# L1 weights quantised tile by tile during the L0 stages; expert weights through a ring of two tiles

## The chip, the cores and the metric

The kernel runs on one core of one Trainium2 chip. The metric is the device time of one execution in microseconds (us), the median of three runs. Five engines work at once: TensorE (PE) multiplies and transposes, VectorE (DVE) and GpSimd (POOL) do elementwise work and reductions, ScalarE (ACT) does activations and copies, SyncE (SP) issues every DMA.

## The reference

A four-layer pre-norm decoder in fp32: batch 8, sequence 128, width 256, 16 heads. Each layer is an attention, a cross-attention (or another mixer) and a feed-forward part, each added to `x`. What matters here:

```python
# L0 feed-forward: hidden width 1024, plain fp32
gated = jax.nn.silu(x @ w_gate.T) * (x @ w_up.T);  out = gated @ w_down.T

# L1 feed-forward: weights and activations on shared exponents, blocks of 32
amax = max(abs(xb), axis=-1)                  # of one block of 32
scale = exp2(clip(floor(log2(amax)) - 2, -127, 127))
q = quantize_elem(xb / scale) * scale         # 2 exponent bits, saturated
out = _mx_linear(silu(_mx_linear(x, w_gate)) * _mx_linear(x, w_up), w_down)

# L2 feed-forward: 8 experts, the best 2 of each token, rank-32 additions
x1 = x @ W1.T + lora1;  x3 = x @ W3.T + lora3   # hidden width 896
x2 = silu(x1) * x3
out += (x2 @ W2.T + lora2) * rw[:, k:k + 1]     # k = 0, 1
```

The weights of the L1 feed-forward part are 1024x256, 1024x256 and 256x1024, 3 MB in all, and they depend on no activation: they can be quantised at any time after they are loaded.

## The kernel before

The work is cut into small **units** (`rows`, `cols`, `pv`, `gate0`, `mg` and so on), each with a part on one or more engines. Batches 0 to 3 form stream A, batches 4 to 7 stream B, loads and work on weights stream W. The twelve stages (L0, L0x, L0F, L1, L1x, L1F, L2, L2x, L2F, L3, L3x, L3F: attention, cross part and feed-forward of each layer) follow each other within a stream. `half()` lists the units of A or B, `weights()` those of W, and the string `TURNS` merges the three lists: `A3` takes the next three units of A, `a4` takes one that lies a few places ahead. Every engine runs its parts of all units in that one order and never out of it, so a unit that waits holds back everything behind it on that engine. Semaphores are counted by `Marks` (`inc`, `at`), buffers that are used in turn by `Ring` (`take` gives the next buffer and what must have ended, `done` frees it). `put` and `get` issue DMAs, all on SP's queue.

**L1 weight units.** `load l1f0`, `l1f1`, `l1f2` fetch the three weights into `wB` (10 DMAs, after `down L0F 3`, the last unit of the L0 feed-forward part: the space was that part's). `mxw(n, k)` quantises one of 12 tiles of 128x512 on DVE (`mx_quant`, ten instructions: a maximum over blocks, five small ones of 128x16, four of 128x512), then two additions on POOL (`mx_out`) round it to bf16, four transposes on PE (`mxw_t`) and a copy on ACT put it into `mgT`, `muT` or `mdT`. These units stand between those of the L1 attention of both halves. The scratch `mxw_w` holds one tile's two intermediates, the small rings `mxw_s`, `mxw_l` two tiles.

**Attention units.** A `rows` unit computes scores of 128x512 on PE (with the causal mask as a matmul with `cmask`) and their maxima on DVE (`negm`); `nm` sends the negated maxima by DMA into `stkA` or `stkB`; `cols` computes the scores again, transposed, with the maximum subtracted, for the exponential on ACT; `pv` multiplies by the values. For L0 the stacks are filled by `stack0` (queries or keys, DMA out of `scrq`, `scrk`) and `mrow` (the mask row out of `scrm`, which exists once `down L0 1` has run, and constant rows).

**L2 feed-forward units.** `w13(hf, f)` loads one tile of 512 KB (four DMAs: W1, W3, B1, B3 of 128 hidden units) into a ring of three tiles in `wB`, after `mxd 7`, the last product of the L1 part. `mg(hf, f)` multiplies with it (8 matmuls of 128x512, two records each in the trace), `ms(hf, f)` adds the second expert's difference and frees the tile. `w2` (896 KB) lies whole in `wA`, loaded by `l2n` after the L1 feed-forward part, and is read by `mw`.

## Time and profile before

| what | value |
|---|---|
| median of 3 runs | 1195.68 us (1198.04, 1195.68, 1180.78) |
| the profiled execution | 1184.46 us, its span 1182.6 us |
| PE busy | 972.1 us, 82% of the span |
| DVE busy | 769.7 us, 65% |
| ACT busy | 387.6 us, 33% |
| POOL busy | 295.8 us, 25% |
| DMA | 79.59 MB, mean 67 GB/s |

The profile is of one execution. Busy time is the time in which an engine had an instruction in it; PEclk is the clock that TensorE was granted, in tenths of full speed; in a row of the timeline the first number is the start, the second the duration, and in square brackets stands how long the engine had been idle and what ended it.

### The profile page before, as it was taken

What the parts mean: (1) busy time and instruction counts of PE and PEld (TensorE: products, weight loads), DVE (VectorE), ACT (ScalarE), POOL (GpSimd) and SP (SyncE); (2) the same over time, 40 slices, a digit from 0 to 9 for tenths busy, and PEclk for the clock granted to TensorE, in tenths of its full rate; (3) what the DMA queues carried; (4) which work ended last, traced back from release to release, by engine and by line L of the source; (5) the groups of instructions that cost most, each with busy time, mean ns of one, the idle gap of its engine ahead of it and who ended that gap; (6) DMA issues with size and microseconds to landing.
All of it is one profiled execution on the core that took longest, in us unless ns stands there. A gap on an engine that the chain in (4) does not pass through costs nothing.

```text
span 1182.6 us, 16030 instructions
## 1 busy us (share of the span) xinstructions
PE 972.1 (82%) x5874; PEld 577.6 (49%) x5878; DVE 769.7 (65%) x1764; ACT 387.6 (33%) x766; POOL 295.8 (25%) x314
## 2 busy tenths in 40 slices
PE   6677999999978676635736689999999999896778
PEld 3333344455745454313414554554644447584667
DVE  6783688424299899899789772523432214898786
ACT  2213477612135334413424341351212302413121
POOL 2420000101034243243023343112332322360520
PEclk9865699999999798766868789999999999998989
DMA  8686500001774445400170266112101140450001
GB/s 277 97 135 130 62 2 3 1 1 43 122 187 85 79 82 118 81 1 2 42 121 2 75 155 114 38 37 82 37 0 54 36 87 2 155 106 2 2 1 36
DMA packets 88065, 79.59 MB, mean 67 GB/s; under 512 B 8968, under 2 KB 86449, under 8 KB 87730
## 3 DMA queue, kind: packets, MB, share of 16 engines
q1 hardware_dynamic: 87986, 78.56, 31.4%
q8 instruction: 47, 0.77, 0.3%
q14 instruction: 32, 0.25, 0.1%
HBM read 62.41 MB, written 15.60 MB: 66 GB/s over the span
## 4 chain that ended last, share of the span: by engine, by line
PE 56%; DVE 28%; DMA 6%; issue 5%; ACT 3%; SPq 1%; POOL 1%; DVEq 0%; POOLq 0%; ACTq 0%
PE bank L562 52%; DVE negm L1406 5%; DMA stkA<-nm 2%; DMA stkB<-nm 1%; DMA stkA<-scrq 1%; PE bank L576 1%; PE bank L690 1%; SPq L1988 1%; ACT E L1126 1%; DVE hr L1327 1%; DVE nm L1426 1%; DVE oT L1806 1%; DVE nmb L1424 1%; DVE mxs L1569 1%; DVE stkB L1800 1%
## 5 line engine op out<-in xcount | busy, mean ns | idle before, releaser
L1406 DVE TENSOR_REDUCE negm<-bank 128x2 f32<-128x512 f32 (+1 forms) x256 | 163.0, 685 | 46.1 <-PE bank L562 44.6
L1126 ACT ACTIVATE E<-bank 128x512 f32<-128x512 f32 x256 | 140.7, 599 | 119.5 <-PE bank L562 117.9
L562 PE MATMUL bank<-hT,wB 128*128 128x512 f32 x272 | 126.0, 605 | 0.0
L1886 POOL TENSOR_TENSOR rstd<-ve,mhalf 128x2 f32<-128x2 f32 x48 | 35.1, 732 | 334.3 <-DVE ve L1319 334.2
L562 PE MATMUL bank<-stkA 96*128 96x128 bf16 (+5 forms) x768 | 93.8, 274 | 24.4 <-DMA stkA<-nm 14.0
L562 PE MATMUL bank<-E,vaug 128*32 128x128 f32 (+1 forms) x1536 | 97.7, 345 | 16.4 <-ACT E L1126 14.3
L562 PEld LDWEIGHTS bank<-stkA 96*128 96x128 bf16 (+5 forms) x768 | 61.6, 108 | 68.7 <-issue 32.2
L562 PE MATMUL bank<-stkB 96*128 96x128 bf16 (+5 forms) x768 | 83.4, 248 | 13.7 <-DMA stkB<-nm 5.4
L562 PEld LDWEIGHTS bank<-hT,wB 128*128 128x128 f32 x272 | 51.6, 194 | 60.1 <-issue 59.3
L562 PEld LDWEIGHTS bank<-stkB 96*128 96x128 bf16 (+5 forms) x768 | 57.8, 102 | 47.2 <-issue 21.9
L562 PE MATMUL bank<-wB 128*128 128x512 f32 x168 | 75.8, 594 | 0.0
L562 PE MATMUL bank<-hT,wA 128*128 128x512 f32 (+1 forms) x120 | 58.4, 638 | 2.1 <-ACT hT L1098 2.1
L1098 ACT COPY hT<-bank 128x512 f32<-128x512 f32 x36 | 21.0, 587 | 118.6 <-PE bank L576 118.6
L562 PEld LDWEIGHTS bank<-E,vaug 128*32 128x32 f32 x1536 | 33.9, 113 | 52.8 <-issue 23.3
L576 PE MATMUL bank<-ident,hr 128*128 128x128 f32 x144 | 24.5, 301 | 32.6 <-DVE hr L1327 32.6
L562 PEld LDWEIGHTS bank<-wB 128*128 128x128 f32 x168 | 31.4, 190 | 37.0 <-issue 36.8
L562 PE MATMUL bank<-stkA,wA 128*128 128x256 f32 (+1 forms) x152 | 47.8, 473 | 0.0
L1739 DVE TENSOR_TENSOR stkA<-E,bank 128x512 f32<-128x512 f32 x14 | 9.6, 687 | 57.9 <-PE bank L562 35.0
L562 PE MATMUL bank<-wA,oT 128*128 128x256 f32 (+2 forms) x192 | 43.5, 365 | 4.3 <-ACT oT L1149 3.3
L562 PE MATMUL bank<-stkB,wA 128*128 128x256 f32 (+1 forms) x152 | 47.0, 471 | 0.0
L562 PE MATMUL bank<-wB,oT 128*128 128x256 bf16 (+1 forms) x124 | 34.3, 439 | 14.2 <-DVE negm L1406 4.5
L1739 DVE TENSOR_TENSOR stkB<-E,bank 128x512 f32<-128x512 f32 x14 | 9.6, 688 | 55.3 <-PE bank L562 35.4
(302 smaller groups left out, 1846.2 us busy)
## 6 DMA issues: line engine op xcount, KB each, us to landing
scrq<-parts SPq DMA_DIRECT2D x20, 384.0 KB, 2.6
scrk<-parts SPq DMA_DIRECT2D x16, 384.0 KB, 2.8
wB<-in_l_w SPq DMA_DIRECT2D x28, 128.0 KB, 2.4
wB<-in_l_b SPq DMA_DIRECT2D x28, 128.0 KB, 2.4
stkA<-scrq SPq DMA_DIRECT2D x4, 768.0 KB, 8.8
stkA<-scrk SPq DMA_DIRECT2D x6, 512.0 KB, 9.8
stkB<-scrq SPq DMA_DIRECT2D x4, 768.0 KB, 8.6
stkB<-scrk SPq DMA_DIRECT2D x6, 512.0 KB, 9.4
```

Of the source, the lines that this page charges most:

```text
L562: return e.matmul(out, lhsT, rhs, start=start, stop=stop, skip_group_check=True)
L576: i = e.transpose(bk[:, k * 256 + c * 128:k * 256 + c * 128 + 128], HR.buf((L, p))[:, k, c * 128:c * 128 + 128], ident[:, :])
L690: i = e.transpose(bk[:, q * 128:q * 128 + 128], ut[:, s:s + 128], ident[:, :])
L1098: e.copy(hT_pair(hT, p), banks.buf(("feat", L, p))[:, :].rearrange("q (b c t) -> q b c t", b=2, c=2)).then_inc(*inc("hT", L, p))
L1126: e.activation(eb[:, :], banks.buf(("cols", L, b, u))[:, :], ACT.Exp, scale=8 ** -0.5 if L == "L0x" else 0.25).then_inc(*inc("exp", L, b, u))
L1327: e.tensor_scalar(hp[:, k, :], x[:, b, :], mv[:, b, 0:1], rstd[:, b:b + 1], ALU.subtract, ALU.mult).then_inc(*inc("norm", L, b))
L1406: e.tensor_reduce(ng[:, o:o + hp], banks.buf(("rows", L, b, u))[:, :].rearrange("p (h s) -> p h s", h=hp), AX, ALU.max, negate=True).then_ ...
L1424: e.tensor_copy(rb, r).then_inc(*inc("maxb", L, b))
L1426: e.tensor_tensor(nm[64:80, 0:n], r, rb, ALU.subtract).then_inc(*inc("maxl", L, b))
L1569: e.tensor_reduce(a, s3, AX, ALU.max, apply_absolute_value=True).then_inc(*inc("mxa", *key, 0))
L1739: e.tensor_tensor((X0, X1)[k][hf][:, f, :], eb[:, :], banks.buf(("mg", hf, f, 1))[:, :], ALU.mult).then_inc(*inc("xk", hf, f, k))
L1886: e.tensor_tensor(rstd[:, 2 * p:2 * p + 2], ve[:, 2 * p:2 * p + 2], mhalf[:, 2 * p:2 * p + 2], ALU.pow).then_inc(*inc("rstd", L, p))
```

## The change

- The loads `l1f0` to `l1f2` are gone. A new unit `l1f(n, k)` loads one tile of 256 KB into a ring `XW` of two tiles in `oT`, the buffer of the L0 cross-attention's context; it waits for the last readers of that context and for the tile's transposes. `mxw` reads the ring, `mx_out` writes into it, `mxw_t` frees it. The scratch lies in `oT` too, and the small rings have one entry each instead of two.
- In the merged order all 12 tiles move from the L1 attention to the end of the L0 cross-attention of B and the L0 feed-forward part of both halves. The order has been written anew throughout; other things in it move as well (the first stacks, the loads `l1a` and `l1x`, the int8 weights' units, ten `rows` of L1).
- `mgT`, `muT` lie at the end of `wB`, `mdT` in `wA`. ACT's copies into `oT` in L1 wait for the last tile, the `q8t` copies of the queries wait for `down L1`.
- `W13` is a ring of two tiles with memory of its own; `w13` and `a13` wait for `down L0F 3` instead of `mxd 7`. `w2` is no longer kept whole: it goes through the same ring for each half, as two units of 4 and 3 row blocks, and `mw` waits for them.

```diff
         steps += [[(u, bs[n - d]) for u in us] for d, us in ((0, ("x2s", "x2e")), (1, ("x2t",)), (2, ("x2o",))) if 0 <= n - d < 4]
     out["L2x"] = steps
-    steps = [[("w13", 0, f)] for f in range(3)] if hf == 0 else []
+    steps = [[("w13", hf, f)] for f in range(2)]
     steps += layernorm("L2F", ps) + [[("lg", hf), ("rt", hf)], [("lgT", hf)], [("mk", hf)]]
     steps += [[("ma", hf, n, c)] for n in range(2) for c in range(2)] + [[("mg", hf, 0)]]
     for f in range(1, 8):
         steps += ([[("mg", hf, f)]] if f < 7 else []) + [[("ms", hf, f - 1)]]
-        steps += [[("w13", hf, f + 2)]] if f < 5 else [[("w13", 1, f - 5)]] if hf == 0 else []
+        steps += [[("w13", hf, f + 1) if f < 6 else ("w2", hf, f - 6)]]
     steps += [[("ma2", hf, k, c)] for k in range(2) for c in range(2)] + [[("zf", hf, f)] for f in range(7)]
     out["L2F"] = steps + [[("mw", p)] for p in ps] + [[("mb", p)] for p in ps]
     out["L3"] = head("L3", hf) + attention("L3", bs)
...
-    out += [("L1", [("load", "l1a")])] + [("L1x", [("load", n)]) for n in ("l1x", "l1xb", "l1bq")]
-    out += [("L1x", s) for n in range(2) for s in ([("q8w", n)], [("q8w_t", n), ("q8w_d", n)], [("q8w_s", n)])]
+    out += [("L1", [("load", n)]) for n in ("l1x", "l1a", "l1bq", "l1xb")]
+    out += [("L1", s) for n in range(2) for s in ([("q8w", n)], [("q8w_t", n), ("q8w_d", n)], [("q8w_s", n)])]
     mxw = [(n, k) for n in range(3) for k in range(4)]
-    out += [("L1F", [("load", f"l1f{n}")]) for n in range(3)] + [("L1F", [("mxw", *mxw[0])])]
-    for i in range(1, 12):
-        out += [("L1F", [("mxw", *mxw[i])]), ("L1F", [("mxw_t", *mxw[i - 1])])]
-    out += [("L1F", [("mxw_t", *mxw[11])]), ("L2", [("load", "l2a")])]
+    out += [("L1", [("l1f", *mxw[n])]) for n in range(2)]
+    for i in range(12):
+        out += [("L1", [("mxw", *mxw[i])]), ("L1", [("mxw_t", *mxw[i])])]
+        out += [("L1", [("l1f", *mxw[i + 2])])] if i < 10 else []
+    out += [("L2", [("load", "l2a")])]
...
 TURNS = """
-W6 w6 w6 w6 W3 A3 a1 B1 W2 B1 W1 A3 a1 A3 a1 a2 a2 a2 a2 a4 a4 A1 a3 a3 a3 A1 a2 W1 a2 W1 B1 b4 a2 a2 A1 B1 b4 a1 B2
...
+W11 w1 w1 w1 A3 W1 a1 B2 A3 a1 A2 a4 A1 a1 a2 a2 a2 a4 a4 a4 a4 A2 a2 a2 a2 a2 W1 a2 W1 B1 b4 a2 B2 b3 B1 a2 a2 B2 a3
...
-        mgT = wB[:, 7168:8192].bitcast(BF).rearrange("p (c f) -> p c f", c=2)
-        muT = wB[:, 0:1024].bitcast(BF).rearrange("p (c f) -> p c f", c=2)
-        mdT = wB[:, 1024:2048].bitcast(BF).rearrange("p (c f) -> p c f", c=8)
-        W13 = Ring(m, [wB[:, 1024 * n:1024 * n + 1024].rearrange("p (w c f) -> p w c f", w=4, c=2) for n in range(3)])
-        a1, a3 = a2(wB[:, 3072:3584], 2), a2(wB[:, 3584:4096], 2)
-        w2, a2w, b2 = a2(wA[:, 2048:3840], 7), a2(wA[:, 3840:5632], 7), a2(wA[:, 5632:6144], 2)
+        mgT, muT = (wB[:, 1024 * n:1024 * n + 1024].bitcast(BF).rearrange("p (c f) -> p c f", c=2) for n in (6, 7))
+        mdT = wA[:, 2048:3072].bitcast(BF).rearrange("p (c f) -> p c f", c=8)
+        W13 = Ring(m, [wB[:, 1024 * n:1024 * n + 1024] for n in range(2)])
+        a1, a3 = a2(wB[:, 2048:2560], 2), a2(wB[:, 2560:3072], 2)
+        a2w, b2 = a2(wA[:, 3072:4864], 7), a2(wA[:, 5632:6144], 2)
...
-        mxw_s = Ring(m, [va[0][:, 1152 + 16 * n:1168 + 16 * n] for n in range(2)])
-        mxw_l = Ring(m, [a2(va[0][:, 1184 + 32 * n:1216 + 32 * n], 2) for n in range(2)])
-        mxw_w = Ring(m, [wB[:, 6144 + 512 * n:6656 + 512 * n] for n in range(2)])
+        mxw_s, mxw_l = Ring(m, [sc[:, 1, 48:64]]), Ring(m, [a2(sc[:, 0, 32:64], 2)])
+        mxw_w = Ring(m, [oTf[:, 512 * n:512 * n + 512] for n in range(2)])
+        XW = Ring(m, [oTf[:, 512 * n:512 * n + 512] for n in (2, 3)])
...
-        a1s, a3s = oT, wB[:, 4096:5120].rearrange("p (c t) -> p c t", c=2)
+        a1s, a3s = oT, wB[:, 3072:4096].rearrange("p (c t) -> p c t", c=2)
         MK = [[[va[h][:, 272 + 256 * (2 * k + c):528 + 256 * (2 * k + c)].bitcast(BF) for c in range(2)] for k in range(2)]
               for h in range(2)]
-        AM = [[wB[:, 5120 + 1024 * n + 512 * c:5632 + 1024 * n + 512 * c] for c in range(2)] for n in range(2)]
+        AM = [[wB[:, 4096 + 1024 * n + 512 * c:4608 + 1024 * n + 512 * c] for c in range(2)] for n in range(2)]
...
             def mxw_t(n, k):
                 bk = take(("mxw_t", n, k))
                 w.wait_ge(*at("mxo", "w", n, k))
-                bb = bk[:, 0:256].bitcast(BF)
-                out = wB[:, 2048 * n + 512 * k:2048 * n + 512 * k + 256].bitcast(BF)
+                bb, out = bk[:, 0:256].bitcast(BF), XW.buf((n, k))[:, 0:256].bitcast(BF)
                 for q in range(4):
                     o = q % 2 * 256 + q // 2 * 128 if n < 2 else q * 128
                     i = e.transpose(bb[:, o:o + 128], out[:, q * 128:q * 128 + 128], identb[:, :])
                 i.then_inc(*inc("mxw_t", n, k))
+                XW.done((n, k), "mxw_t", n, k)
...
-                        mm(bk[:, k * 256:k * 256 + 256], X0[hf][:, f, j * S:j * S + S], w2[:, f, :],
-                           k == 0 and f == 0, False)
+                        w.wait_ge(*at("w2", hf, f // 4))
+                        i = mm(bk[:, k * 256:k * 256 + 256], X0[hf][:, f, j * S:j * S + S],
+                               W13.buf(("w2", hf, f // 4))[:, 256 * (f % 4):256 * (f % 4) + 256], k == 0 and f == 0, False)
+                i.then_inc(*inc("mw", p))
+                if p % 2 == 1:
+                    for n in range(2):
+                        W13.done(("w2", hf, n), "mw", p)
...
             def oTt(L, b):
+                if L == "L1":
+                    w.wait_ge(*(at("mxw_t", 2, 3) if b // 4 else at("mxo", "w", 2, 3)))
                 w.wait_ge(*at("oTt", L, b))
...
+                if kind == "q":
+                    w.wait_ge(*at("down", "L1", b // 4 * 2 + 1))
...
+                w.wait_ge(*at("srow"))
+                w.wait_ge(*at("q8r", 1))
...
-                w.wait_ge(*at("load", f"l1f{n}"))
-                mx_quant((mxw_s, mxw_l, mxw_w), wB[:, 2048 * n + 512 * k:2048 * n + 512 * k + 512], 16, 1, 6.0, ("w", n, k))
+                w.wait_ge(*at("z", "L0x", "k", 1))
+                w.wait_ge(*at("l0v", 3))
+                w.wait_ge(*at("l1f", n, k))
+                mx_quant((mxw_s, mxw_l, mxw_w), XW.buf((n, k)), 16, 1, 6.0, ("w", n, k))
...
-                if hf == 1:
-                    w.wait_ge(*at("am2", 0, 1))
+                w.wait_ge(*(at("am2", 0, 1) if hf else at("down", "L0F", 3)))
...
-                mx_out(wB[:, 2048 * n + 512 * k:2048 * n + 512 * k + 256].bitcast(BF), mxw_w, 16, ("w", n, k))
+                mx_out(XW.buf((n, k))[:, 0:256].bitcast(BF), mxw_w, 16, ("w", n, k))
...
-                elif name in ("l1f0", "l1f1", "l1f2"):
-                    n = int(name[3])
-                    w.wait_ge(*at("down", "L0F", 3))
-                    for k in range(4 if n < 2 else 2):
-                        k0, k1 = (256 * k, 2) if n < 2 else (128 * k, 1)
-                        o = 2048 * n + (512 if n < 2 else 1024) * k
-                        get(a2(wB[:, o:o + (512 if n < 2 else 1024)], k1),
-                            a2_rows(IN["l1_w" + ("g", "u", "d")[n]][k0:k0 + 128 * k1]))
...
                 elif name == "a13":
-                    w.wait_ge(*at("mxd", 7))
+                    w.wait_ge(*at("down", "L0F", 3))
                     get(a1, src2("l2_a1"))
                     get(a3, src2("l2_a3"))
                 elif name == "l2n":
-                    w.wait_ge(*at("x", "L1F", 7))
-                    for dst, n in ((w2, "w2"), (a2w, "a2"), (b2, "b2")):
+                    for b in range(B):
+                        w.wait_ge(*at("x", "L1x", b))
+                    for dst, n in ((a2w, "a2"), (b2, "b2")):
                         get(dst, src2("l2_" + n))
...
+            def l1f(n, k):
+                dst, freed = XW.take((n, k))
+                for s in freed:
+                    w.wait_ge(*s)
+                w.wait_ge(*at("z", "L0x", "k", 3))
+                w.wait_ge(*at("l0v", 7))
+                wt = IN["l1_w" + "gud"[n]]
+                put(a2(dst, 2 if n < 2 else 1), a2_rows(wt[256 * k:256 * k + 256] if n < 2 else
+                                                        wt[128 * (k // 2):128 * (k // 2) + 128, 512 * (k % 2):512 * (k % 2) + 512]),
+                    "l1f", n, k, sem=f"d_l1f{XW.index((n, k))}")
             def w13(hf, f):
                 key = (hf, f)
                 dst, freed = W13.take(key)
                 for s in freed:
                     w.wait_ge(*s)
-                w.wait_ge(*at("mxd", 7))
+                w.wait_ge(*at("down", "L0F", 3))
                 for k, n in enumerate(("w1", "w3", "b1", "b3")):
-                    put(dst[:, k, :, :], src2("l2_" + n)[:, :, f * 128:f * 128 + 128], "w13", hf, f,
-                        sem=f"d_w13{W13.index(key)}")
+                    put(dst.rearrange("p (w c f) -> p w c f", w=4, c=2)[:, k, :, :],
+                        src2("l2_" + n)[:, :, f * 128:f * 128 + 128], "w13", hf, f, sem=f"d_w13{W13.index(key)}")
+            def w2(hf, n):
+                key = ("w2", hf, n)
+                dst, freed = W13.take(key)
+                for s in freed:
+                    w.wait_ge(*s)
+                r = 4 - n
+                put(a2(dst[:, 0:256 * r], r), a2_rows(IN["l2_w2"][512 * n:512 * n + 128 * r]), *key,
+                    sem=f"d_w13{W13.index(key)}")
```

The order of SP at the start, from the second key to the query stack of L0 (`stkA` is A's stack; 8x16x512 and 16x16x512 are the key stack of two batches, 24x16x512 the query stack; `scrm` and `in_c_one` are the mask row and the constant rows). Before:

```order
L1988 DMA scrm<-wA 1x2048
L1988 DMA stkA<-scrk 8x16x512 x2
L1988 DMA stkA<-scrk 16x16x512 x2
L1988 DMA scrq<-parts 128x3x512
L1988 DMA stkA<-scrk 8x16x512 x2
L1988 DMA stkA<-scrk 16x16x512 x2
L1988 DMA stkA<-scrm 1x16x512
L1988 DMA stkA<-in_c_one 3x16x512
L1988 DMA stkA<-in_c_one 1x16x512
L1988 DMA stkA<-scrq 24x16x512
```

And of the change:

```order
L2004 DMA scrm<-wA 1x2048
L2004 DMA scrq<-parts 128x3x512
L2004 DMA stkA<-scrm 1x16x512
L2004 DMA stkA<-in_c_one 3x16x512
L2004 DMA stkA<-in_c_one 1x16x512
L2004 DMA stkA<-scrk 8x16x512 x2
L2004 DMA stkA<-scrk 16x16x512 x2
L2004 DMA stkA<-scrk 8x16x512 x2
L2004 DMA stkA<-scrk 16x16x512 x2
L2004 DMA stkA<-scrq 24x16x512
```

The mask row and the query projection's store now stand ahead of the first key stack.

The order of DVE where L0x of B ends and the L0 feed-forward part of A begins (L1585 to L1605 are the ten instructions of one `mxw`, L1497 is the product of gate and up of the L0 part), of the change:

```order
L1585 TENSOR_REDUCE sc<-oT 128x16
L1587 TENSOR_SCALAR sc<-sc 128x16
L1589 TENSOR_SCALAR sc<-sc 128x16
L1592 TENSOR_SCALAR sc<-sc 128x16
L1593 TENSOR_SCALAR sc<-sc 128x16
L1595 TENSOR_SCALAR sc<-sc 128x16
L1599 TENSOR_TENSOR oT<-oT,sc 128x512
L1600 TENSOR_SCALAR oT<-oT 128x512
L1603 TENSOR_TENSOR oT<-oT,sc 128x512
L1605 SCALAR_TENSOR_TENSOR oT<-oT,sc 128x512
L1497 TENSOR_TENSOR stkA<-E,bank 128x512
```

Before, the same products of the L0 part (there L1481) follow each other with nothing of the kind between them, and the first tile comes in L1, behind the first `nm`:

```order
L1481 TENSOR_TENSOR stkA<-E,bank 128x512 x3
L1327 TENSOR_SCALAR hr<-x,mv,rstd 128x256 x2
L1367 TENSOR_TENSOR x<-x,bank 128x512
...
L1406 TENSOR_REDUCE negm<-bank 128x4
L1420 TENSOR_TENSOR nmt<-bank,nm 16x128
L1424 CAST nmb<-nmt 16x128
L1426 TENSOR_TENSOR nm<-nmt,nmb 16x128
L1569 TENSOR_REDUCE vaug<-wB 128x16
L1571 TENSOR_SCALAR vaug<-vaug 128x16
```

So each tile's ten instructions now stand ahead of a product on which a later unit of PE waits.

The order of PE in the L0 feed-forward part, of the change (`hT,wB` 128x512 x4 is one `gate0` product, `identb,oT` the transposes of one tile, `cmask` and `stkA` one `rows` of L1):

```order
L865 MATMUL bank<-identb,oT 128x128 x4
L564 MATMUL bank<-hT,wB 128x512 x12
L865 MATMUL bank<-identb,oT 128x128 x4
L564 MATMUL bank<-hT,wB 128x512 x8
L865 MATMUL bank<-identb,oT 128x128 x4
L564 MATMUL bank<-wB,stkB 128x256 x16
L865 MATMUL bank<-identb,oT 128x128 x4
L564 MATMUL bank<-cmask,identb 128x512
L564 MATMUL bank<-stkA 128x128 x4
```

Before, the transposes stand in groups of three tiles between the units of the L1 attention:

```order
L864 MATMUL bank<-identb,wB 128x128 x12
L748 MATMUL bank<-ident,ot 128x128 x2
L562 MATMUL bank<-cmask,identb 128x512
L562 MATMUL bank<-stkA 128x128 x4
```

Between two tiles' transposes PE now has one to three products of L0.

## Rows read from the trace of the kernel before

**Rows 1.** Busy time by stretch of the program, with the granted clock.

```profile
core 0: us, PE busy (x) PEld busy (x) DVE busy (x) ACT busy (x) POOL busy (x), PEclk, DMA share, GB/s
65.00:70.00 5.00, 0.00 (x0) 0.00 (x0) 3.88 (x13) 0.00 (x0) 4.45 (x7) 1.00 0.46 71
97.00:142.00 45.00, 42.02 (x270) 16.64 (x271) 24.01 (x45) 20.23 (x38) 0.00 (x0) 0.50 0.67 99
142.00:216.00 74.00, 69.07 (x712) 35.10 (x710) 62.52 (x135) 51.85 (x100) 1.91 (x2) 1.00 0.01 3
216.00:328.00 112.00, 110.58 (x462) 64.93 (x462) 36.61 (x92) 29.60 (x54) 8.89 (x12) 1.00 0.27 51
328.00:437.00 109.00, 80.69 (x722) 50.85 (x722) 100.83 (x237) 45.63 (x97) 40.92 (x39) 0.91 0.53 107
437.00:673.00 236.00, 139.63 (x1214) 86.72 (x1218) 210.52 (x489) 84.31 (x165) 72.35 (x59) 0.78 0.26 50
725.00:1000.00 275.00, 271.27 (x1107) 144.68 (x1109) 89.53 (x216) 70.77 (x138) 70.85 (x62) 1.00 0.17 44
```

**Rows 2.** What VectorE waited for from 328 to 673 us, longest.

```profile
DVE tmp L1633 <- PE bank L562: 3.8, 2, 2.8
```

**Rows 3.** VectorE, busy with the tiles in wB alone: start:end, width, busy (instructions).

```profile
333.00:442.00 109.00, 34.83 (x60) 0.91 0.51 95
```

**Rows 4.** Groups of VectorE instructions, 333 to 442 us: maxima, and small ones.

```profile
L1406 DVE TENSOR_REDUCE negm<-bank 128x4 f32<-128x512 f32 x23 | 14.7, 684 | 0.2
...
L1573 DVE TENSOR_SCALAR vaug<-vaug 128x16 int32<-128x16 int32 x12 | 6.6, 552 | 0.4
...
L1576 DVE TENSOR_SCALAR vaug<-vaug 128x16 f32<-128x16 f32 x12 | 4.0, 330 | 0.4
L1571 DVE TENSOR_SCALAR vaug<-vaug 128x16 f32<-128x16 f32 x12 | 3.6, 298 | 0.4
...
L1579 DVE TENSOR_SCALAR vaug<-vaug 128x16 f32<-128x16 f32 x12 | 2.1, 175 | 0.4
...
L1577 DVE TENSOR_SCALAR vaug<-vaug 128x16 f32<-128x16 f32 x12 | 2.0, 167 | 0.0
```

**Rows 5.** Timeline, VectorE, one tile's small instructions.

```profile
342.04 1.08 DVE L1573 TENSOR_SCALAR vaug<-vaug 128x16 int32<-128x16 int32 x1
```

**Rows 6.** Timeline, GpSimd, around the same time.

```profile
338.72 1.27 POOL L1925 TENSOR_TENSOR wB<-wB 128x512 bf16<-128x512 f32 x1
340.82 3.38 POOL L1900 TENSOR_TENSOR parts<-tmp,parts 128x512 bf16<-128x512 f32 x3 [0.83 <-ACT parts L1121]
```

**Rows 7.** Timeline, TensorE: transposes of three tiles.

```profile
361.33 0.83 PE L864 MATMUL bank<-identb,wB 128*128 128x128 bf16 x12
```

**Rows 8.** Groups of TensorE instructions, 328 to 437 us.

```profile
L562 PE MATMUL bank<-cmask,identb 128*128 128x512 bf16 x56 | 23.7, 422 | 5.0 <-DMA stkB<-nm 2.8 <-DVE negm L1406 2.2
```

**Rows 9.** Groups of TensorE instructions, 216 to 328 us.

```profile
L562 PE MATMUL bank<-hT,wB 128*128 128x512 f32 x128 | 56.1, 592 | 0.0
```

**Rows 10.** DMA issues, 325 to 345 us.

```profile
wB<-in_l_wu SPq DMA_DIRECT2D x4, 256.0 KB, 5.0
```

**Rows 11.** DMA issues of the whole page.

```profile
wB<-in_l_w SPq DMA_DIRECT2D x28, 128.0 KB, 2.4
```

**Rows 12.** Timeline, SyncE, start of the first key stack.

```profile
39.49 2.81 SPq L1988 DMA_DIRECT2D stkA<-scrk  x4
...
50.43 0.60 SPq L1988 DMA_DIRECT2D stkA<-scrm  x1
```

**Rows 13.** Timeline, TensorE: first units behind a DMA.

```profile
71.01 3.14 PE L562 MATMUL bank<-stkA 49*128 49x256 bf16 x14 [6.11 <-DMA stkA<-scrq]
...
97.78 1.44 PE L562 MATMUL bank<-stkA 51*128 51x256 bf16 x6 [6.06 <-DMA stkA<-nm]
```

**Rows 14.** Timeline, TensorE: matmuls of the expert part.

```profile
724.28 5.31 PE L562 MATMUL bank<-wB 128*128 128x512 f32 x12
```

95 lines of the change are left out of this document (49 added, 46 removed).

## Prediction, made before the changed kernel had run

> **What bounds the kernel now.** I read the busy time by stretch first [rows 1]. From 328 to 437 us (the L1 attention of both halves, with all 12 tiles of L1 weights among it) DVE is busy 100.8 of 109 us and PE 80.7. From 437 to 673 us (L1x, L1F, the start of L2) DVE is busy 210.5 of 236 us, PE 139.6. The longest waits of DVE in these 345 us are two of together 3.8 us [rows 2]. So DVE sets the pace there: a microsecond less of DVE is up to a microsecond less of time. In the L0 feed-forward part, 216 to 328 us, it is the other way round: PE 110.6 of 112 us at clock 1.00, DVE only 36.6, POOL 8.9. The expert part, 725 to 1000 us, is PE's too: 271.3 of 275. The reader is to see that the change carries DVE work from a stretch that lacks DVE into one that has 75 us of it idle.
>
> **The tiles.** What lies in `wB` (five instructions of 128x512 a tile, 60 in all) keeps DVE busy 34.8 us [rows 3], the five small ones of 128x16 take 6.6 + 4.0 + 3.6 + 2.1 + 2.0 = 18.3 us [rows 4]. Together 53.1 us, 4.4 a tile. Moved with them across the end of the L0 part are ten maxima of L1 `rows` at 0.68 us [rows 4] and small work of their norm, by the merged order's count about 8.5 us. So the 345 us lose 53 + 8.5 = some 61.5 us of DVE.
>
> **Why not 61.5 us of time.** By the order, up to the last `cols` of the L1 attention DVE loses 51 us: 100.8 becomes about 50. PE then has the most to do: 80.7 less the transposes (0.83 us for twelve, 3.3 for 48 [rows 7]), less ten `rows` of about 0.43 us (a `cmask` matmul is 0.42, the four others run nearly beside it [rows 8]), plus what moves up from later, gives 75 us. The nearest stretch of attention in which DVE is not the bound is 142 to 216 us: PE 69.1 of 74 us, clock 1.00 [rows 1]. At that share 75 us take 81; I add 3 for a clock a little under 1.00 (0.91 now), so 84: **−25 us**. Bounds: 77 (PE nearly without gaps, −32) and 95 (waits for `nm` and `ot` as now, −14). Behind it DVE has about 13 us less to do (the last tile, norm and `rows` work of L1x that the new order draws forward); at DVE's share of 0.89 that would be 14, but chains of the mx part wait for POOL and PE too: **−11 us**, bounds −5 and −16.
>
> **The L0 feed-forward part.** DVE's 36.6 + 62 us still fit in 112, so the work itself is hidden behind PE's products. PE gets 48 transposes, 3.3 us, and the ten `rows`, 4.3 us, at nothing hidden, because PE is busy 99%. Then the stalls. DVE does a tile ahead of a product of gate and up, and the `down0` behind it waits for that product. One tile's chain: silu and product (128x512 like the maxima, 0.68 each [rows 4]), tile 4.4, POOL 2 x 1.27 [rows 6], an estimated 0.4 of handing over: 8.7 us. Its cover is two `gate0` of 8 matmul records each (128 records in all, their spans overlapping at a mean of 592 ns [rows 9]; twelve such records take 5.31 us [rows 14], so 3.5 us a `gate0`) and small work, 8 us together. Where it repeats, each tile can cost 0.7 us. The ring of two tiles reloads in 5.0 us (256 KB, [rows 10]) behind the transposes; one entry of scratch makes DVE wait for POOL's 2.5 us only where two tiles stand together, which is at the end of L0x. I take 4 us of stalls, from 0 to 12. Sum **+12 us**, from +8 to +20.
>
> There is one gain that I don't count. The small instructions are slow in bursts: one of 128x16 took 1.08 us at 342.04 [rows 5], while POOL ran from 340.82 for 3.38 us [rows 6]; the same size takes 0.167 us in another group [rows 4]. The Trainium skill, "SBUF — State Buffer", "Who interferes with whom", says that VectorE and GpSimd take an exclusive lock on a shared port and the loser stalls fully; the trace agrees as far as these two rows go. In the L0 part POOL is busy 8.9 of 112 us instead of 40.9 of 109 [rows 1], so a tile may cost 3.7 us (34.8/12 + 5 x 0.17) in place of 4.4: 8 us of DVE less, where DVE is not the bound. The sum is the same with and without it; it only shortens the chain above to below its cover.
>
> **The start.** SP's order now has the mask row ahead of the first key stack. That row waits for `scrm`, which went out at 50.43 us with nothing in its way [rows 12], while the first key stack was issued at 39.49. So its DMAs (four at 2.81 us of issue) come ten microseconds later, behind each other with the second stack's. The first `rows` of PE, at 71.01 us after a wait of 6.11 for the query stack [rows 13], can only come later, by about 5 to 7 us; but the next point, the `cols` at 97.78 after 6.06 us of waiting for `nm` [rows 13], had slack, and the `l1a` load that ran ahead of it on the queue is now behind it. **+2 us**, from 0 to +8.
>
> **The expert part.** A tile of `w13` is reloaded once `ms(f−1)` has ended and must be there for `mg(f+1)`. Between them lie `mg(f)` (16 records, 7 us by [rows 14]) and `ms(f)` (8, 3.5 us): 10 us of PE, against four issues of some 2.8 us [rows 12] and 2.4 of landing [rows 11], 5 to 6 us. Slack of 4 us, and less where B's stacks share the queue at the first tiles: 0 to 5. `w2` loads behind `ms(5)` and `ms(6)` and is needed only after four `ma2`. The waits for `mxd 7` that go had ended long before `mg`. **+2 us**. If the cover failed at all 14 tiles by 2 us, that would be +28; PE's 99% busy and the distance above speak against it. ACT's new waits (copies into `oT` for the last tile, `q8t` for `down L1`) ask for units that stand well ahead of them: 0.
>
> **Sum.** +2 + 12 − 25 − 11 + 2 = −20 us on the profiled execution's 1184.5 us: 1164.5. That execution is 11 us faster than the median of the three runs and 5.6 faster than the mean of the four times shown (1198.04, 1195.68, 1180.78, 1184.46 give 1189.7). Against the median I add half, 5.5: **1170 us**, 2.1% under 1195.7.
>
> **The rivals.**
> 1. *DVE's full gain.* L1 attention in 77 us (−32), behind it −16, L0 part +10, others 0: −38, so 1146.5 + 5.5 = 1152 us. For it: DVE waits of only a few us; against: PE there is at 0.74 now and never above 0.93 in an attention stretch. Chance 0.18.
> 2. *The clock at the start.* From 97 to 142 us PE is busy 42.0 of 45 us at a granted clock of 0.50 (the level of 1.2 GHz); it had done nothing from 65 to 70 us [rows 1]. If the new order ends this state 36 us earlier, 36 us of work take 18: 1152 us. The Trainium skill, "TensorE: Matmul & The Clock Gate", Part 1, says that activity releases the clock and idle gaps throttle it again; the row of 97 to 142 us, busy and still at 0.50, agrees only in part. Since the wait for the stack stays or grows, chance 0.07.
> 3. *PE-bound in another place.* L1 attention only falls to 95 us, the rest −8, L0 part +20, start +2, experts +2: 1184.5 + 2 = 1186.5 + 5.5 = 1192 us, no change. For it: PE waits for `nm` (DMA) and maxima are latencies that don't shrink with DVE's load. Chance 0.22.
> 4. *Slower: PE stalls in L0F lower its clock.* The L0 part holds 110.6 us of PE at 1.00. Were a wait for tile or ring of the size seen at 71.01 (6.1 us) to come before it, and half of it run at 0.50, that costs 55 us: 1225. It decides from 50 us on. Against: the waits I find are under a microsecond each. Chance 0.10.
>    That the change does not do what it says (tiles not hidden) would be 53 us back in the L0 part; DVE's 75 idle us exclude it but for rival 3.
>
> **The numbers.** Forecast 0.43 (own range 1158 to 1182), rivals 0.18, 0.07, 0.22, 0.10. 2% is about what a measurement here can tell: faster is under 1171.8, slower over 1219.6. Of the forecast's chance a little over half is faster: 0.24 + 0.18 + 0.07 = 0.49; within 0.19 + 0.22 = 0.41; slower 0.10. The range reaches to rivals 1 to 3 and their edges: 1145 to 1200, leaving out rival 4 and some 0.07 of the fast tail.
>
> **What the profile after would show.** Tiles in the L0 part: DVE near 95 of some 124 us, PE still above 0.93. L1 attention: DVE near 50, PE above 0.85, width 80 to 90 us. If its width is over 95, step two fails; if PE waits for POOL or for copies of tiles in the L0 part over 4 us, the stall term does. First `rows` of PE at 76 to 78 us. The small instructions of a tile near 0.2 us. PE in the expert part still above 97%, with no wait for `w13`. The forecast is wrong altogether if the granted clock of the L0 part falls below 1.00, or if the 0.50 stretch at the start moves.

## The result, and the profile after

The changed kernel takes 1244.91 us (median of four runs, 1241.89 to 1248.47), the kernel before 1196.86 (1180.78 to 1198.77): a ratio of 1.045, 95% interval 1.034 to 1.056. I had forecast 1170 us with a range from 1145 to 1200. It is slower by 48 us. The profiled executions, 1246.37 us and 1184.46 us, lie 62 us apart, because the profiled one of before is one of its quicker ones; what follows goes by their traces, so it has to explain 62 us. Ratios and their intervals are of the quicker executions of each kernel: of 71 of the kernel before 69 took 1181 to 1202 us, one 1211 and one 1661, and the time follows the mean granted clock of the execution (1184.65 us at 0.887, 1201.99 at 0.872).

The page's first line, and its row of the granted clock in 40 equal slices:

```profile
PE 1021.1 (82%) x5878; PEld 593.5 (48%) x5878; DVE 776.5 (62%) x1764; ACT 383.1 (31%) x760; POOL 294.5 (24%) x314
PEclk9865755598999979866866769999999999997889
```

DVE has as much work as before (it had 769.7 us), PE is busy 49 us longer with the same matmuls: it ran slower. The mean granted clock is 0.848 instead of 0.895. As one of two levels (1.2 and 2.4 GHz) at any time, 0.848 of 1244.6 us are 378 us at the lower one, against 248 us before.

Where the time went is told by the same unit in both traces. The table gives, for some units, how much later they start on PE than in the kernel before (which starts them at the time in the second column, counted like the rows of a timeline), in us; the other columns are experiments, told of below.

| unit on PE | before | changed | start of after alone | start of before | SP's order | L0x and L3 of before |
|---|---|---|---|---|---|---|
| first `rows0` | 71.0 | +12.9 | +11.5 | 0.0 | +2.7 | +0.7 |
| first `cols0` | 97.8 | +25.0 | +23.4 | +0.6 | +2.4 | +2.8 |
| `cols0`, batch 4 | 171.9 | +40.0 | +44.7 | +1.2 | +18.8 | +11.8 |
| `cols0`, batch 6 | 200.2 | +53.3 | +52.9 | +11.1 | +32.8 | +11.8 |
| last `pv0` | 225.4 | +64.3 | +52.9 | +21.8 | +43.8 | +37.1 |
| last `down0` | 316.4 | +73.1 | +52.9 | +30.5 | +53.1 | +44.8 |
| last `cols` of L1 | 436.2 | +56.5 | +53.7 | +12.6 | +33.6 | +25.5 |
| last `mx_down` | 670.3 | +47.7 | +52.2 | +2.6 | +25.4 | +17.2 |
| last `mw` | 992.5 | +52.0 | +52.7 | +9.6 | +29.4 | +21.4 |
| `rows` of L3, batch 5 | 1063.5 | +64.8 | +52.7 | +22.5 | +42.3 | +20.8 |
| last `down3` of B | 1170.3 | +62.0 | +52.9 | +19.2 | +39.1 | +22.3 |

So of the changed kernel's 62 us, 53 are lost by the time of batch 6's `cols0` in L0x, before any tile is quantised. The stretch with the tiles (to the last `down0`) costs 20 more, the L1 attention gives back 17, L1x to L2 9 more, the expert part costs 4, L3 and its neighbours 10: 53 + 20 − 17 − 9 + 4 + 10 is 61, the difference but for rounding.

**The start.** SP's timeline and PE's, each with start, duration and, in brackets, idle time and what ended it:

```profile
86.40 0.38 SPq L2004 DMA_DIRECT2D scrq<-parts  x1
86.83 5.42 SPq L2004 DMA_DIRECT2D stkB<-scrk  x8
92.30 5.25 SPq L2004 DMA_DIRECT2D stkA<-scrq  x3
99.46 1.99 SPq L2004 DMA_DIRECT2D stkA<-nm  x1
```

```profile
83.86 10.94 PE L564 MATMUL bank<-stkA 49*128 49x256 bf16 x46 [8.45 <-DMA stkA<-scrq]
```

```profile
122.74 1.65 PE L564 MATMUL bank<-stkA 51*128 51x256 bf16 x7 [17.03 <-DMA stkA<-nm]
```

The store `scrq<-parts` of the second query projection stands ahead of B's key stacks now. It waits for DVE's work behind the first maxima of `rows0`. It is no later than before (86.40 us against 87.65); new is what stands behind it: both key stacks of B, 1.5 MB, which went out from 75.13 us before, and then the second query stack of A. `nm`, a few KB on which the first `cols0` waits, follows at 99.46. Before, PE waited 6.06 us there [rows 13]. The place on the queue is only a part of that. The values of `nm` are ready 13.1 us later, because `rows0` starts 12.9 us later; the first two rows are of the kernel before, the third is of the changed one:

```profile
85.89 0.41 DVE L1415 TENSOR_TENSOR nm<-bank,nm 16x256 bf16<-16x256 f32 x1
88.16 1.19 SPq L1988 DMA_DIRECT2D stkA<-nm  x2
98.96 0.41 DVE L1431 TENSOR_TENSOR nm<-bank,nm 16x256 bf16<-16x256 f32 x1
```

So `nm` is issued 11.3 us later, as soon as it is there, and from its issue to the first `cols0` 23.3 us pass instead of 9.6, while 2.3 MB of stacks move ahead of it: 11.3 + 13.7 are the 25 us of the table.

**L0x at the lower clock.** Busy time by stretch (columns as in the rows ahead of the prediction), changed kernel:

```profile
97.00:142.00 45.00, 22.55 (x138) 9.22 (x139) 17.08 (x34) 12.76 (x23) 2.95 (x3) 0.59 0.69 87
142.00:216.00 74.00, 69.51 (x437) 29.48 (x436) 44.04 (x95) 32.51 (x61) 1.81 (x2) 0.56 0.31 39
255.00:388.00 133.00, 126.78 (x602) 70.33 (x602) 87.97 (x223) 46.21 (x85) 38.24 (x35) 0.95 0.29 60
388.00:492.00 104.00, 84.76 (x726) 56.59 (x725) 58.48 (x142) 41.05 (x87) 15.51 (x20) 0.90 0.50 93
492.00:717.00 225.00, 145.36 (x1196) 86.57 (x1194) 201.38 (x460) 82.89 (x162) 65.74 (x53) 0.73 0.28 56
```

From 142 to 216 us PE is as busy as before in that stretch (69.51 us against 69.07), but gets 437 matmul records done instead of 712, at a clock of 0.56 instead of 1.00 [rows 1]. That is the rest of the 53 us. The clock is back at 1.00 from 137 us on and falls again at 151, behind a wait of PE:

```profile
150.81 1.86 PE L564 MATMUL bank<-stkB 49*128 49x256 bf16 x8 [2.98 <-issue]
```

The profile names nothing that ended this wait; the unit is the first `rows0` of B, whose query stack goes out at 139.29 us only. The clock then stays at 0.50 until 243 us. The third to fifth rows answer to the tiles, the L1 attention and what follows it: 133, 104 and 225 us against 112, 109 and 236 [rows 1], with borders that fit to the units only roughly.

### The profile page after: what moved, and what is told of

The parts are those of the page before. It is cut to its first block, busy times and chain, and to the rows that moved or that the text cites. A ratio compares the mean times of both kernels' runs of the same rounds, so it can differ in the third digit from the quotient of the medians.

```text
span 1244.6 us, 16078 instructions
## 1 busy us (share of the span) xinstructions
PE 1021.1 (82%) x5878; PEld 593.5 (48%) x5878; DVE 776.5 (62%) x1764; ACT 383.1 (31%) x760; POOL 294.5 (24%) x314
## 4 chain that ended last, share of the span: by engine, by line
PE 61%; DVE 22%; DMA 5%; issue 4%; ACT 4%; SPq 2%; POOL 2%; DVEq 0%; POOLq 0%; ACTq 0%
PE bank L564 56%; DVE negm L1422 3%; DMA stkA<-scrq 2%; SPq L2004 2%; PE bank L692 2%; DMA stkA<-nm 2%; ACT E L1136 2%; PE bank L578 2%; DVE wA L1809 1%; DVE mxs L1585 1%; DVE hr L1343 1%; DVE stats L1330 1%; DVE mxs L1587 1%; DVE stkB L1817 1%; DVE oT L1823 1%
## 5 line engine op out<-in xcount | busy, mean ns | idle before, releaser
L564 PE MATMUL bank<-stkA 99*128 99x128 bf16 (+5 forms) x768 | 102.5, 285 | 36.8 <-DMA stkA<-nm 18.0
L564 PE MATMUL bank<-E,vaug 128*32 128x128 f32 (+1 forms) x1536 | 110.0, 376 | 15.9 <-ACT E L1136 15.0
L564 PEld LDWEIGHTS bank<-stkA 99*128 99x128 bf16 (+5 forms) x768 | 64.1, 111 | 86.7 <-issue 54.0
L564 PE MATMUL bank<-stkB 99*128 99x128 bf16 (+5 forms) x768 | 94.6, 273 | 4.0 <-issue 3.0
L564 PEld LDWEIGHTS bank<-stkB 99*128 99x128 bf16 (+5 forms) x768 | 62.3, 109 | 45.1 <-issue 27.9
L564 PE MATMUL bank<-wA,oT 128*128 128x256 f32 (+2 forms) x256 | 58.0, 374 | 12.3 <-ACT oT L1234 4.8
L1108 ACT COPY hT<-bank 128x512 f32<-128x512 f32 x36 | 21.1, 588 | 116.2 <-PE bank L578 116.1
L578 PE MATMUL bank<-ident,hr 128*128 128x128 f32 x144 | 29.2, 349 | 31.2 <-DVE hr L1343 31.2
L564 PE MATMUL bank<-stkA,wA 128*128 128x256 f32 (+1 forms) x152 | 47.7, 473 | 5.6 <-issue 4.3
L564 PEld LDWEIGHTS bank<-wA,oT 128*128 128x128 f32 (+1 forms) x256 | 39.1, 172 | 25.8 <-issue 7.9
L1146 ACT CAST nm<-bank 16x128 bf16<-16x128 f32 (+1 forms) x40 | 10.9, 273 | 118.8 <-PE bank L681 118.5
```

Source lines behind the costliest of these rows:

```text
L564: return e.matmul(out, lhsT, rhs, start=start, stop=stop, skip_group_check=True)
L578: i = e.transpose(bk[:, k * 256 + c * 128:k * 256 + c * 128 + 128], HR.buf((L, p))[:, k, c * 128:c * 128 + 128], ident[:, :])
L1108: e.copy(hT_pair(hT, p), banks.buf(("feat", L, p))[:, :].rearrange("q (b c t) -> q b c t", b=2, c=2)).then_inc(*inc("hT", L, p))
```

## The experiments

Each ran beside the kernel before. Where I give a median without a ratio, the runs scatter too much for one.

### The start alone, in the kernel before

The first 300 units of the merged order are the changed kernel's, the rest of the order and all of the code is the kernel before.

```diff
 TURNS = """
-<the merged order of before, units 0 to 299>
+<the merged order of the changed kernel, units 0 to 299>
```

> The kernel before with only the first 300 units of its merged order replaced by those of the changed kernel; tiles, rings and the rest as before. Theory S: the loss comes with the start alone, so 1235 to 1255 us, cols0 of batch 0 at about 122 us, clock 0.50 for some 90 us of L0x. Theory M: 1195 to 1205 us.

Measured: 1236.67 us (ratio 1.034, 1.029 to 1.040). The first `cols0` starts 23 us later, and from there to batch 6's `cols0` 29 us more are lost; behind it the difference moves by about a microsecond at most (the third column of numbers in the table). Its stretches:

```profile
97.00:142.00 45.00, 24.57 (x133) 9.20 (x134) 15.31 (x31) 12.73 (x23) 2.96 (x3) 0.50 0.70 88
142.00:230.00 88.00, 86.53 (x502) 37.17 (x503) 46.20 (x93) 36.81 (x70) 1.22 (x1) 0.50 0.23 31
230.00:330.00 100.00, 96.11 (x616) 51.47 (x615) 51.25 (x128) 45.25 (x84) 8.21 (x11) 0.98 0.01 2
```

With no tile moved and no ring changed, the start makes 41 of the 48 us, and the clock is 0.50 from 97 to 230 us. So most of the loss is made by the start (theory S), and the tiles (theory M) are not needed for it.

### The changed kernel with the start of before

```diff
 TURNS = """
-<the merged order of the changed kernel, units 0 to 299>
+<the merged order of before, units 0 to 299>
```

> The changed kernel with the first 300 units of the merged order (up to the rows of L0x batch 5) put back to the order of before; everything behind them, the tiles, the rings and their memory stay changed. Theory S (the loss is made at the start: the nm transfer of L0x stands behind three stacks on SP's queue, PE waits 17 us for it, and TensorE then runs most of L0x at a granted clock of 0.50): the first cols0 is back at about 98 us, clock 1.00 from 150 us on, and 45 to 50 us of the 48 us loss go, so 1190 to 1200 us. Theory M (the moved tiles themselves cost the time, by DVE, POOL and DMA work in L0x and L0F): 1230 to 1245 us, with the loss showing up only behind 230 us.

Measured: 1207.66 us, ratio 1.012 (1.006 to 1.018). 37 of the 48 us go. A loss of 12 us stays, and the table's column "start of before" shows from where: 10 us within L0x by batch 5, 20 in the stretch of the tiles, −18, −10, +7 in the expert part and +10 in L3.

### `nm` ahead of three stacks

```diff
-... stack0 k 2, stack0 k 3, stack0 q 1, <10 units>, nm L0x 0
+... <10 units>, nm L0x 0, stack0 k 2, stack0 k 3, stack0 q 1
```

> The changed kernel with three units moved, all of them on SP alone: the key stacks of B (768 KB each) and the second query stack of A are issued behind nm of batch 0 instead of ahead of it. Theory S in its narrow form (nm's place on the queue): the wait of 17 us for nm shrinks to under 6, the first cols0 comes at 105 us or earlier, and the time falls by 18 us at least, by up to 50 if TensorE's clock then rises at 140 us as it did before: 1195 to 1227 us. If the order of nm is not the cause but only the late first key stack: no more than 5 us, 1240 to 1245 us.

Measured: 1241.26 us, one of four runs at 1218.39. The first `cols0` came at 103.4 us (+5.6), but then PE waited at the first `rows0` of batch 2, which reads the second query stack, now last on the queue:

```profile
103.96 5.32 SPq L2004 DMA_DIRECT2D stkA<-scrq  x3
```

```profile
132.47 0.58 PE L564 MATMUL bank<-stkA 49*128 49x256 bf16 x2 [16.32 <-issue]
```

The wait of 17 us had become one of 16 us (the row names nothing that ended it; the stack is what the unit needs and had gone out last). `nm`'s place alone was not the cause: the key stacks of B leave 12 us later than before in the changed kernel and 23 us later here, and whatever stands behind them waits.

### SP's order of before at the start

Eight units that run on SP alone go back to their places of before: first stack, then mask row; the load of L1's weights and B's key stacks ahead of the second query store; `nm` ahead of the second query stack. No other engine's order changes.

```diff
-mrow 0, stack0 k 0, stack0 k 1 | mrow 1, l0q 1, sp1 q 1, ..., stack0 k 2, stack0 k 3, stack0 q 1, ..., nm 0 | ..., load l1a
+stack0 k 0, ..., stack0 k 1, mrow 0 | load l1a, mrow 1, stack0 k 2, stack0 k 3, l0q 1, sp1 q 1, ..., nm 0, stack0 q 1
```

> The changed kernel with eight units of the start, all on SP alone (five stacks, two mask rows, the load of the L1 attention weights), put where the order of before has them; no other engine's order changes. Theory S1 (the late stacks and the nm behind them are a matter of SP's queue alone): first cols0 at about 100 us, the wait of 17 us gone and none of 16 us in its place as in the kernel with nm first, and 30 to 48 us less: 1197 to 1215 us. Theory S2 (the units on the computing engines matter as much, the query part of batches 2 and 3 ahead of the rows): not over 15 us less, 1230 us or more.

Measured: 1226.2 us (ratio 1.028, 1.021 to 1.036). It lies between the two theories, and the trace says why: the waits are gone (first `cols0` +2.4 us, batch 1 −0.6), but L0x is slow all the same.

```profile
142.00:149.00 7.00, 6.05 (x53) 2.18 (x52) 6.97 (x12) 1.95 (x4) 0.00 (x0) 0.93 0.17 42
149.00:224.00 75.00, 74.61 (x435) 29.80 (x435) 39.59 (x86) 34.65 (x65) 1.91 (x2) 0.51 0.01 1
```

So the start costs twice: some 20 us through SP's queue, and some 20 through the clock in L0x (+32.8 us by batch 6, where the kernel with the whole start of before has +11.1), which fell with no wait of over 0.82 us shortly ahead of it.

### Useless matmuls in the waits

Into the bank that the unit overwrites anyway:

```diff
+                if (b, u) == (0, 0):
+                    for k in range(20):
+                        mm(bk[:, 0:128], ident[:, :], ident[:, :], True, True)
                 w.wait_ge(*at("stack", "L0x", "k", p))
...
+                if (b, u) == (0, 0):
+                    for k in range(20):
+                        mm(bk[:, 0:128], ident[:, :], ident[:, :], True, True)
                 w.wait_ge(*at("nm", "L0x", b))
```

In the kernel before:

> The kernel before with useless matmuls on PE in its two waits of 6 us, 20 products of ident with ident (fp32, 128x128) ahead of the first rows0's wait and 20 ahead of the first cols0's wait, into the bank that the unit then overwrites; the result is unchanged. Theory C1 (PE standing idle there lets the granted clock fall to 0.50 at 70 us): the clock stays at 1.00 for all or most of 70 to 142 us, PE's 60 us of work there take half, and the time falls by 15 to 35 us, 1162 to 1182 us. Theory C2 (the clock falls and comes back for another reason): the fall stays, and the time is unchanged or up to 6 us longer, 1195 to 1203 us.

In the changed kernel, with 28 and 55 of them:

> The changed kernel with the same useless matmuls, 28 ahead of the first rows0's wait of 8 us and 55 ahead of the first cols0's wait of 17 us. The DMA waits stay as they are. Theory C1: the clock is at 1.00 when the first cols0 starts and stays there through L0x, so the 28 us lost between 123 and 245 us come back: 1205 to 1220 us. Theory C2: clock 0.50 from 150 to 240 us as before, 1240 to 1250 us.

Measured: 1192.22 us beside 1192.99, and 1241.41 us (ratio 1.041, 1.033 to 1.049). Filling a wait does lift the clock while it lasts, but L0x loses it again. The changed kernel so filled:

```profile
100.00:120.00 20.00, 16.52 (x114) 14.30 (x114) 2.33 (x5) 2.50 (x4) 2.28 (x2) 0.88 1.04 103
120.00:140.00 20.00, 19.06 (x126) 7.27 (x126) 9.72 (x15) 9.53 (x18) 0.00 (x0) 0.55 0.31 78
140.00:160.00 20.00, 17.91 (x174) 9.18 (x170) 17.25 (x35) 10.80 (x20) 0.00 (x0) 0.93 1.01 125
160.00:230.00 70.00, 66.95 (x383) 26.71 (x384) 36.65 (x78) 30.68 (x57) 1.91 (x2) 0.50 0.01 4
```

In the first row it is 0.88 where it was 0.59 without the fill. Theory C1 fell as I had put it: the clock was at 1.00 again from 143 to 160 us, so standing idle at the start is not what keeps it down from 160 to 230. But the fill was not whole, and behind it another wait came up. In the same trace both falls in L0x stand behind a wait that was left:

```profile
120.94 2.16 PE L564 MATMUL bank<-stkA 51*128 51x256 bf16 x14 [4.09 <-DMA stkA<-nm]
162.25 1.44 PE L564 MATMUL bank<-stkA 51*128 51x256 bf16 x6 [2.56 <-DMA stkA<-nm]
```

So this run does not speak against waits as the cause of a fall.

### One wait in the middle of L0x, in the kernel before

A first kernel for this, which had the first `cols0` of batch 4 about ten units earlier, gave no result. In its place stand useless maxima on DVE ahead of the subtraction that makes `nm` of batch 4 (six, or two in the second kernel); PE then waits for the bank that this subtraction frees, or for `nm`:

```diff
                 if L == "L0x":
+                    if b == 4:
+                        for k in range(6):
+                            e.tensor_reduce(mxs[:, 0, 4 * k:4 * k + 4],
+                                            banks.buf(("maxT", L, b))[:, :].rearrange("p (h s) -> p h s", h=4), AX, ALU.max)
                     e.tensor_tensor(nm[32:48, 0:n], ...
```

> The kernel before with six useless maxima of 128x512 (0.69 us each, 4.1 us together) on DVE ahead of the one that makes nm of batch 4 in L0x, so that PE, at a clock of 1.00 there, waits some 4 us for that transfer at 170 us. Nothing else changes. Theory C1 (one wait of a few us in L0x lets the granted clock fall and L0x keeps it down): a stretch of 0.50 begins within a few us of 172 us and lasts 20 us or more; 10 to 30 us longer than before, 1204 to 1225 us. Theory C2 (the wait costs itself alone): 1194 to 1199 us, clock 1.00.

> The same with two maxima instead of six, 1.4 us, so that PE waits about 1 us. Theory C1 with a wait of any length: as with six. If the length of the wait decides: no fall, 1193 to 1197 us.

Measured: 1213.81 us with six (ratio 1.019, 1.011 to 1.026), 1197.55 with two (1.002, 0.998 to 1.007); of the twelve executions with two, four took 1209 to 1217 us and do not enter that ratio. The trace with six:

```profile
171.83 0.60 PE L562 MATMUL bank<-stkB 49*128 49x256 bf16 x2 [2.54 <-DVE nm L1419]
```

```profile
142.00:170.00 28.00, 25.77 (x268) 12.88 (x267) 24.06 (x48) 19.35 (x38) 0.00 (x0) 1.00 0.01 2
170.00:174.00 4.00, 2.17 (x13) 0.95 (x14) 3.96 (x8) 0.36 (x1) 0.39 (x1) 0.72 0.02 4
174.00:182.00 8.00, 8.00 (x45) 4.12 (x43) 4.74 (x12) 3.60 (x7) 0.83 (x1) 0.50 0.00 0
```

One wait of 2.54 us at a clock of 1.00, and the clock is 0.50 right behind it, for 20 us, though PE is then busy all the time. In this execution, the quickest of the six (1197.43 us), some 9 us are lost between batch 1 and batch 5 of L0x and hardly any behind them; the median of the six is 20 us over that of the kernel before, and what the other five lost was not traced. Here theory C1 holds, for the fall: a wait of that length in L0x is enough. The kernel with the start of before has one at its joint, 2.68 us for `nm` of batch 4; its clock falls there too, and 11 us are lost.

The kernel with two maxima does not show that a shorter wait costs nothing. In its trace (1208.71 us) the clock, at 0.50 since 70 us, comes back only at 183 us, in an order that up to there is that of the kernel before; then PE waits 0.92 us at 1.00, and the clock falls again, for 17 us:

```profile
142.00:170.00 28.00, 28.00 (x164) 12.46 (x161) 14.90 (x28) 11.23 (x21) 0.00 (x0) 0.50 0.01 2
184.00:187.00 3.00, 2.86 (x32) 1.14 (x34) 2.50 (x5) 2.32 (x6) 0.00 (x0) 1.00 0.00 0
189.03 2.56 PE L562 MATMUL bank<-stkB 51*128 51x256 bf16 x14 [0.92 <-DMA stkB<-nm]
190.00:193.00 3.00, 3.00 (x17) 1.68 (x18) 2.00 (x4) 1.62 (x4) 0.00 (x0) 0.50 0.00 0
```

### Dense matmuls in L0x

```diff
                 w.wait_ge(*at("nm", "L0x", b))
+                if b < 8:
+                    mm(bk[:, 0:256], identb[:, :], cmask[:, :, :].rearrange("p a b -> p (a b)"), True, True)
```

On the kernel with SP's order of before (all 128 units), on the kernel before (`b < 2 and u % 2 == 0`), and on the one with start and tail of before (`u % 2 == 0`):

> The changed kernel with SP's order of before at the start (1226.2 us, granted clock 0.50 from 149 to 225 us though PE is busy the whole time), with one useless dense matmul (128 rows, 128x256, bf16, into the bank that the unit then overwrites) in each of the 128 cols0 units of L0x; nothing else. The units' own matmuls read 49 to 51 rows of 128 or write 32 columns. Theory D1 (a busy PE whose matmuls fill little of the array is not enough to bring the clock back; once a short wait has let it fall, L0x keeps it down): the clock is back at 1.00 soon after each fall, the stretch shrinks by 30 to 35 us against 14 us of filling: 1205 to 1212 us. Theory D2 (what the matmuls fill does not matter): clock 0.50 as before, the filling costs 14 to 27 us: 1240 to 1253 us.

> The kernel before with the same dense matmul in every other cols0 unit of batches 0 and 1 (16 of them), where it runs at 0.50 from 97 to 142 us with PE 93% busy. Theory D1: the clock rises well before 142 us, 10 to 20 us gained, 2 us spent: 1178 to 1188 us. Theory D2: 1195 to 1200 us.

> The changed kernel with start and tail of before (1205.5 us), with the dense matmul in every other cols0 unit (64 of them). It is what is left of the idea with the three losses taken away. Theory D1: L0x at 1.00, 20 us back, 7 us spent, and the terms of my prediction behind it (+9 in L0F, -18 in L1, -10 behind it, +7 in the expert part): 1180 to 1192 us. Theory D2: 1212 to 1220 us.

Measured: 1267.85, 1200.15 (ratio 1.007) and 1245.21 us, beside 1226.2, 1194.46 and 1205.5 without. Theory D1 fell as I had put it: this much dense work among the units does not bring the clock back (whether more would was not tried). The third of them had a clock of 1.00 to 181 us and then, behind a wait of 2.32 us, lost it for 106 us, at a PE that is hardly ever idle:

```profile
142.00:181.00 39.00, 35.87 (x362) 16.82 (x355) 32.72 (x67) 24.11 (x46) 0.19 (x1) 1.00 0.05 7
181.00:287.00 106.00, 104.61 (x552) 40.23 (x552) 50.20 (x115) 43.69 (x81) 7.51 (x7) 0.50 0.03 10
```

### What the tiles are worth

Start and all of L3 from before (341 units behind the last load of `w2`):

```diff
-<units 0 to 299 and the last 341 in the order of the change>
+<units 0 to 299 and the last 341 in the order of before>
```

> The changed kernel with the first 300 units and all units behind the last load of w2 (L3 of both halves, the ternary weights) in the order of before; the tiles, rings and everything between as changed. The comparison is with the kernel whose start alone was put back (1207.7 us). If the loss of 11 us in L3 is made by the new order there (DVE 5.8 to 6.0 of 6 us busy, PE waiting for the ternary weights' mean): 1195 to 1199 us. If it came from something carried over from the expert part: 1206 us or more.

Measured: 1205.52 us (ratio 1.008). The median hardly moved, but the traces do tell: from the last `mw` to the end it loses 0.9 us (+21.1 to +22.0), where the kernel with the start alone put back loses 9.6. PE's waits in that stretch of the changed kernel:

```profile
PE bank L564 <- issue: 4.3, 1, 4.3
PE bank L1061 <- DVE tcol L1792: 4.2, 1, 4.2
PE bank L578 <- DVE hr L1343: 3.8, 1, 3.8
```

`tcol` is the mean for the ternary weights of L3's feed-forward part. With the old order the first two are gone and the third is 2.3 us; the second and the third wait for DVE's work. L0x was slower in this profile (+22 by batch 6 instead of +11, with the same order there), which ate the gain.

Then nearly all of L0x (440 units) and L3 from before:

```diff
-<units 0 to 439 and the last 341 in the order of the change>
+<units 0 to 439 and the last 341 in the order of before, four units on the int8 weights spread over L0x>
```

> The changed kernel with nearly all of L0x (the first 440 units) and all of L3 in the order of before; only four units on the int8 weights are spread over L0x so that no engine waits at the joint. The tiles, the rings and the order from the end of L0x to the end of the expert part are the change's. Expected if the idea is worth what the stretches of the other runs say (start 0, L0F +9, L1 -18, L1x to L2 -10, expert part +5, L3 0, against 1193 to 1197 us of before): 1180 to 1186 us, faster than both kernels. If L0x falls to a granted clock of 0.50 here too, by chance or by the tiles at its end: 1200 to 1210 us.

Measured: 1203.27 us (ratio 1.005, 1.001 to 1.010); its quickest run 1187.97. The clock was at 1.00 from 171 us and fell at 215. No tile is at work there, the first begins at 237.7 us; DVE does the work on the int8 weights that was spread over L0x just before, and PE waits 0.83 us for the maxima behind it:

```profile
213.22 0.39 PE L563 MATMUL bank<-stkB 51*128 51x256 bf16 x2 [0.83 <-DVE negm L1421]
97.00:171.00 74.00, 69.04 (x421) 28.62 (x421) 38.66 (x72) 31.01 (x58) 0.00 (x0) 0.50 0.41 65
171.00:215.00 44.00, 40.35 (x428) 19.95 (x429) 38.08 (x82) 31.57 (x61) 1.22 (x1) 1.00 0.01 3
215.00:260.00 45.00, 43.61 (x237) 17.98 (x236) 23.92 (x65) 20.86 (x40) 6.47 (x6) 0.51 0.07 19
```

Last, the tiles moved in the order of before, the whole of it:

```diff
-<W's units: loads l1f0 to l1f2 and all mxw, mxw_t within L1>
+<l1f, mxw, mxw_t and the int8 weights' units at the change's places in L0x and L0F; w13, w2 behind the ms that frees a tile>
```

> The idea of the change on the order of before: memory, rings, the tiles (and the int8 weights' units) at the places that the change gives them between the units of L0x and L0F, the loads of expert tiles by the ring of two; every unit of both halves in the order of before (but one ms that the smaller ring asks for, and w13, w2). My prediction's terms for this without the start: +12 in L0F, -25 in L1, -11 behind it, +2 in the expert part, so about -22: 1175 us. The rival (latencies of nm and maxima hold the L1 stretch, the L0F part pays in full): 1190 to 1205 us. Theory M: 1230 us and more.

Measured: 1255.6 us (1233.43 to 1266.97; ratio 1.040, 1.029 to 1.051). Of the 75 us that its trace is longer, 37 are lost by batch 6 in L0x, before the first tile at 252.8 us: its first `cols0` is 1.7 us late, and it is at 0.50 without a break until 210 us, in an order that differs from that of before up to unit 300 in the units on the int8 weights alone.

```profile
97.00:142.00 45.00, 40.38 (x254) 16.21 (x258) 21.73 (x39) 18.72 (x36) 0.00 (x0) 0.50 0.67 101
142.00:210.00 68.00, 66.83 (x396) 28.33 (x392) 38.00 (x80) 29.91 (x57) 1.22 (x1) 0.50 0.01 2
```

The other 38 are not the start's: 24 in the stretch of the tiles, −9 in the L1 attention, +16 from there to the last `mx_down`, +7 in the expert part. In the order of before the tiles thus cost more than they give back; why was not looked into.

No version beats the kernel before by more than the runs scatter.

## Why the prediction was wrong

**The start, "+2 us, from 0 to +8": 53 us.** This is the step that failed. I had seen the first `rows0` come later (I said 5 to 7 us, it was 12.9: the first query stack goes out at 59.64 us, 7.1 later than before, and its issue takes 6.87 us instead of 2.18) and then wrote that the next point, the `cols0`, "had slack". It had none: PE waited 6.06 us for `nm` there already [rows 13], and a point that is waited for has no slack. I also took the load `l1a` off the queue ahead of `nm`, but did not follow what B's key stacks now wait for. They stand behind a store of the second query projection that leaves at 86.40 us, and with them 2.3 MB leave just ahead of `nm`. That is 25 us at the first `cols0`: 11 because `nm` is made and sent later, 14 because it lands later.

**The clock in L0x.** I gave the clock two rivals, and both in the wrong place: one that the 0.50 of 70 to 142 us ends earlier (0.07), and the slower one, that waits lower the clock in the feed-forward part (0.10). The mechanism of the slower one was right, the fall behind a wait of few microseconds; that its 1225 us lies nearest of all to the result is luck, for it put 55 us on the L0 feed-forward part, which kept its clock, and it was L0x that lost it, for 28 us of time, beside 25 us at the start that this rival did not have. The rows of before did hold a hint: from 97 to 142 us PE was busy 42 of 45 us and still at 0.50 [rows 1]. I noted this and did not draw the conclusion that in L0x a lost clock can stay lost for long. I had also written that the forecast would be "wrong altogether" if that stretch moves; that is what happened.

**The tiles, "+12 us, from +8 to +20": 20 us.** The transposes, the ten `rows` and the stalls were about right: PE's waits for POOL's part of a tile are 0.6 us in all, and from the last `pv0` to the last `down0` 9 us are lost. The other 11 are lost at the end of L0x, where the first tiles stand, a place that I had left out: there DVE is still needed for L0x itself. PE waits 1.60 us behind the second tile, at a clock of 1.00, and the clock is 0.50 for 10 us:

```profile
276.88 1.08 PE L564 MATMUL bank<-E,vaug 128*32 128x256 f32 x8 [1.60 <-ACT E L1136]
```

The tiles did get cheaper, as said: the small instruction that took 552 ns [rows 4] takes 174 now, and the five together 11.7 us instead of 18.3.

```profile
L1592 DVE TENSOR_SCALAR sc<-sc 128x16 f32<-128x16 f32 x12 | 3.0, 253 | 0.4
L1587 DVE TENSOR_SCALAR sc<-sc 128x16 f32<-128x16 f32 x12 | 2.5, 206 | 0.4
L1589 DVE TENSOR_SCALAR sc<-sc 128x16 int32<-128x16 int32 x12 | 2.1, 174 | 0.4
```

With POOL busy 29% of the time from 255 to 388 us instead of 38%, that agrees with what the Trainium skill, "SBUF — State Buffer", "Who interferes with whom", says of a port that VectorE and GpSimd share; that POOL is the cause was not tried.

**The L1 attention, "−25 us": −17.** The row of 388 to 492 us begins earlier in the program than my 328 to 437. With borders at the same units, from the last `down0` to the last `cols` of L1, before and then changed:

```profile
317.00:437.00 120.00, 91.14 (x796) 59.33 (x795) 105.76 (x248) 46.22 (x98) 42.16 (x41) 0.91 0.50 104
390.00:493.00 103.00, 84.46 (x728) 56.11 (x728) 57.39 (x140) 41.80 (x87) 15.12 (x19) 0.90 0.51 94
```

DVE lost 48.4 us (said: 51), PE lost 6.7 (said: 5.7), and PE became the bound, as said. The term that was off is PE's share: I had 75 of 84 us, 0.89, taken from a stretch at full clock; it is 84.5 of 103, 0.82. PE has waits for `nm`, `wA` and `ot` there (3.9, 7.6 and 2.0 us) at which the clock dips. At 0.89 the stretch would be 95 us and the gain 25. **Behind it, "−11 us": −9.** Right.

**The expert part, "+2 us": +4.** No wait for a tile of `w13` shows among PE's waits there; the ring of two is hidden, and the size was right within its bounds.

**L3, not in the sum: +10.** The prediction has no term for L3, and gives no reason for leaving it out. The order there was new, and PE waits for DVE's part of it.

Two slips in the sum moved nothing: the mean of the four times is 5.3 us over the profiled execution, not 5.6, and 75 us at the share 69.1/74 are 80.3, not 81.

By these stretches the idea itself is worth 17 + 9 − 20 − 4, 2 us, in the order of the change: the 53 us of DVE that L1 no longer has come back as 26 us there, and 24 of them are spent ahead of and behind it. My sum for the same four terms was −22. No run shows the 2 us by themselves, and in the order of before the same four add up to a loss of 38.

**What stays open.** Over all traces of this case, between 97 and 300 us, PE began 17 waits of 1.5 us or more (up to 4.09) at a clock of 1.00 or just under it, and behind each of them the clock was 0.50; of 17 waits of 0.7 to 1.3 us, 5 had a fall behind them and 12 had none, the two of the kernel before (0.83 and 0.81) among these. So in this stretch a wait of 1.5 us or more was always followed by a fall, but why some short ones do and others do not is not settled, nor why it fell in the kernel with SP's order of before, behind four waits of 0.21 to 0.32 us and one of 0.82. What keeps it at 0.50 for 17 or 20 us in one run and for 92 or 106 in another, with PE busy nearly all the time, and what ends it, was not found either. Orders that are the same up to that point had it back at 142 us (before; start of before), 170 (start and tail of before), 171 and 183 (before with two maxima), so a part of it varies from run to run without any change of the program. Dense matmuls between the others did not bring it back.

## What to carry to other kernels

Where an engine waits for a small transfer, ask what stands ahead of it on the queue and what that waits for in its turn, and when its own values are ready: the point has no slack, and every large transfer that is released late lands on it. Where the granted clock of a stretch is low though TensorE is busy, treat the stretch as one in which a wait of a few microseconds may cost several times its length (9 us for 2.54 and 11 for 2.68 here; behind 2.98 us the changed kernel was at half clock for 92 us), and price a reordering there with that. And an order that was written anew has to be read to its end: 10 of these 62 us were lost in a stage that the change does not speak of.

## What was not expected of the hardware

- One wait of 2.54 us of TensorE, at a granted clock of 1.00, was followed by 20 us at 0.50 with TensorE busy 8.00 of 8 us in the middle of it; the traced execution lost 9 us by it, and the median rose by 20 us for 4.1 us of work.
- TensorE stayed at 0.50 for 106 us while it was busy 104.61 of them. The Trainium skill, "TensorE: Matmul & The Clock Gate", Part 1, lets activity release the clock; in these rows a busy engine alone did not.
- From the issue of a transfer of a few KB to the matmul that waited for it 23.3 us passed behind 2.3 MB on the same queue, against 9.6 us before.
- In an order that did not differ up to there, the stretch of 0.50 that begins at 70 us ended at 142 us in one execution and at 183 us in another.
